# Two attention phases of a Trainium2 kernel: the score matmuls of a pair of heads on separate 64-row halves of the TensorE array

## The reference

```
q, k, v = heads(x @ Wq), heads(x @ Wk), heads(x @ Wv)     # 16 heads, width 8
scores  = q @ k.T / sqrt(8)          # layer 0: q, k turned by rope first
scores  = scores - slope[h] * (j - i), -inf where j > i   # layer 2 only
out     = softmax(scores) @ v
x       = x + out @ Wo
```

## Time and profile before

| what | value |
|---|---|
| time, median of 3 runs | 6658.86 us (6647.43 to 6664.04) |
| profiled execution, span from first to last instruction | 6645.5 us |
| TensorE matmul busy | 4915.4 us (74%) |
| VectorE busy | 4210.3 us (63%) |
| ScalarE busy | 2311.0 us (35%) |
| GpSimd busy | 1627.5 us (24%) |
| `rotary`: s1 of the first sequence to the last s2 | 205.6 to 1323.8 us |
| `alibi`: the same | 3910.1 to 4778.7 us |

### The profile page before, as it was taken

The page is one execution under the profiler, slowest core; times in us unless marked ns, Lnnn a source line. Parts: engine busy times, 40 slices in busy tenths (PEclk is TensorE's granted clock), DMA queues, the critical chain, the costliest instruction groups (busy, mean ns, idle before and its releaser), DMA issues. The chain is left out here.

```text
span 6645.5 us, 116690 instructions
## 1 busy us (share of the span) xinstructions
PE 4915.4 (74%) x40300; PEld 2948.5 (44%) x40521; DVE 4210.3 (63%) x9351; ACT 2311.0 (35%) x4383; POOL 1627.5 (24%) x1976
## 2 busy tenths in 40 slices
PE   3699999857671165675666649889766799897998
PEld 2233333233341154443334424444344577665776
DVE  7566666478897511487889846656499455455554
ACT  2366656620240001543001115555511344201443
POOL 1443333220233200033014423333244110001110
PEclk8899999988885555866777769999977899866999
DMA  1211121000132333410000022222000000000000
GB/s 37 45 41 36 34 44 32 17 5 0 38 120 77 75 93 75 90 33 28 0 0 0 0 41 52 47 47 47 17 0 0 18 0 0 1 0 0 1 0 26
DMA packets 230189, 202.36 MB, mean 30 GB/s; under 512 B 23551, under 2 KB 203863, under 8 KB 229335
## 3 DMA queue, kind: packets, MB, share of 16 engines
q1 hardware_dynamic: 229783, 196.88, 12.8%
HBM read 118.68 MB, written 72.88 MB: 29 GB/s over the span
## 5 line engine op out<-in xcount | busy, mean ns | idle before, releaser
L507 DVE TENSOR_REDUCE rotary_maxima<-rotary_ps_s 128x2 f32<-128x1024 f32 x512 | 616.6, 1220 | 418.0 <-PE rotary_ps_s L681 416.5
L730 ACT ACTIVATE rotary_probs<-rotary_ps_s 128x512 f32<-128x512 f32 x1024 | 555.5, 595 | 388.9 <-PE rotary_ps_s L697 373.9
L507 DVE TENSOR_REDUCE alibi_maxima<-alibi_ps_s 128x2 f32<-128x256 f32 (+3 forms) x512 | 412.4, 821 | 372.3 <-PE alibi_ps_s L684 369.2
L2017 DVE SCALAR_TENSOR_TENSOR x<-moe_ps_out,moe_weights,x 128x128 f32 (+1 forms) x1024 | 285.5, 344 | 461.0 <-PE moe_ps_out L2058 433.4
L2058 PEld LDWEIGHTS moe_ps_out<-w_moe_w,moe_hidden 128*128 128x128 f32 x4096 | 495.1, 192 | 108.5 <-issue 80.7
L730 ACT ACTIVATE alibi_probs<-alibi_ps_s 128x512 f32<-128x512 f32 (+3 forms) x1024 | 402.0, 439 | 344.9 <-PE alibi_ps_s L700 339.9
L2058 PE MATMUL moe_ps_out<-w_moe_w,moe_hidden 128*128 128x128 f32 x4096 | 500.6, 275 | 0.0
L2045 PE MATMUL moe_ps_hidden<-moe_z,w_moe_w 128*128 128x512 f32 x1024 | 490.0, 601 | 0.0
L2107 ACT ACTIVATE moe_hidden<-moe_ps_hidden,w_moe_b 128x512 f32<-128x512 f32 x512 | 345.4, 687 | 361.8 <-PE moe_ps_hidden L2045 350.2
L897 PE MATMUL moe_ps_experts<-w_moe_w,moe_normedT 128*128 128x512 f32 x512 | 302.3, 742 | 131.6 <-DVE moe_others L865 131.6
L697 PE MATMUL rotary_ps_s<-rotary_q_stack,rotary_k_stack 128*128 128x512 bf16 x1017 | 339.3, 392 | 30.5 <-ACT rotary_probs L730 7.3
(11 more groups left out here) (446 smaller groups left out, 10659.6 us busy)
## 6 DMA issues: line engine op xcount, KB each, us to landing
rotary_parts<-rotary_part SPq DMA_DIRECT2D x96, 128.0 KB, 2.2
rotary_q_stack<-rotary_parts SPq DMA_DIRECT2D x192, 64.0 KB
rotary_k_stack<-rotary_parts SPq DMA_DIRECT2D x192, 64.0 KB
convolve_bands<-in_filters SPq DMA_DIRECT2D x192, 64.0 KB, 2.7
alibi_parts<-alibi_part SPq DMA_DIRECT2D x96, 128.0 KB, 2.2
alibi_q_stack<-alibi_parts SPq DMA_DIRECT2D x192, 64.0 KB
alibi_k_stack<-alibi_parts SPq DMA_DIRECT2D x192, 64.0 KB
delta_n<-convolved SPq DMA_DIRECT2D x16, 256.0 KB, 2.0
```

The costliest lines, as they stand in the source:

```text
L507: v.tensor_reduce(maxima[:, blk, 2 * pair:2 * pair + 2], ps_s1[t % 2][:, :, 0:keys_of(blk)], AXIS.X, ALU.max).then_inc(s.max_made, 1)
L730: nc.scalar.activation(probs[u % 8][:, 0:T - lo], ps_s2[m][:, 0:T - lo], ACT.Exp).then_inc(s.exp_made, 1)
L2017: v.scalar_tensor_tensor(xb, ps_out[e % 2][:, b:b + 1, :], weights[par][:, b, e:e + 1], xb, ALU.mult, ALU.add).then_inc(s.added, 1)
```

## The change

The query stack gets one column block for each pair, like the key stack, with one head in rows 0 to 63 and the other in rows 64 to 127. Each score matmul of s1 and s2 then reads only the 64 rows of its head, from both stacks. In the causal phase s1's order changes: both heads' scores first, then both masks. The masks, pv and all items keep the full 128 rows. The loads into the query stack write the same bytes to adjacent blocks instead of every second block, and the stack is half as large.

```diff
-    qs = [ph.sb(f"q_stack{j}", [P, HEADS, T], BF16) for j in range(3)]
+    qs = [ph.sb(f"q_stack{j}", [P, PAIRS, T], BF16) for j in range(3)]
...
-                            to, part = ((qs[j][row:row + HD, two::2, :], Q_PARTS[n]), (ks[j][row:row + HD, :, :], K_PARTS[n]))[a]
+                            to, part = ((qs[j][row:row + HD, :, :], Q_PARTS[n]), (ks[j][row:row + HD, :, :], K_PARTS[n]))[a]
...
-                v.tensor_copy(qs[j][:], q_rows[:].unsqueeze(2).broadcast_to([P, HEADS, T])).then_inc(s.stack_set, 1)
+                v.tensor_copy(qs[j][:], q_rows[:].unsqueeze(2).broadcast_to([P, PAIRS, T])).then_inc(s.stack_set, 1)
...
                         for two in range(2):
-                            last = mm(ps_s1[t % 2][:, two, 0:n], qs[jb][:, 2 * pair + two, blk * P:(blk + 1) * P],
-                                      ks[jb][:, pair, 0:n], start=True, stop=not causal)
-                            if causal:
+                            rows = slice(two * ROWS, (two + 1) * ROWS)
+                            last = mm(ps_s1[t % 2][:, two, 0:n], qs[jb][rows, pair, blk * P:(blk + 1) * P],
+                                      ks[jb][rows, pair, 0:n], start=True, stop=not causal)
+                        if causal:
+                            for two in range(2):
                                 last = mm(ps_s1[t % 2][:, two, n - P:n], w.ident16, w.later_keys, start=False, stop=True)
...
+                        pair = 2 * qd + t % 2
                         for m in range(2):
-                            h = 4 * qd + 2 * (t % 2) + m
+                            rows = slice(m * ROWS, (m + 1) * ROWS)
...
-                            last = mm(ps_s2[m][:, 0:T - lo], ks[jc][:, h // 2, kb * P:(kb + 1) * P], qs[jc][:, h, lo:T],
+                            last = mm(ps_s2[m][:, 0:T - lo], ks[jc][rows, pair, kb * P:(kb + 1) * P], qs[jc][rows, pair, lo:T],
                                       start=True, stop=not causal)
```

More of the change, by code:

```diff
@@ L396, in attention @@
     oT = ph.sb("oT", [C, T])
-    q_rows = ph.sb("q_rows", [P, HEADS])
+    q_rows = ph.sb("q_rows", [P, PAIRS])
     carrier = ph.sb("pool_carrier", [1, 13])
@@ L437, in load_stack @@
                             row = two * ROWS + SHIFT_ROW
-                            sp.dma_start(qs[j][row:row + 3, two::2, :], zeros[:].rearrange("r (p t) -> r p t", t=T)).then_inc(s.stack_loaded, 16)
+                            sp.dma_start(qs[j][row:row + 3, :, :], zeros[:].rearrange("r (p t) -> r p t", t=T)).then_inc(s.stack_loaded, 16)
                 def store_shift(half):
@@ L448, in load_shift @@
                         row = two * ROWS + SHIFT_ROW
-                        sp.dma_start(qs[(j - 1) % 3][row:row + 3, half * PAIRS + two:(half + 1) * PAIRS:2, :],
+                        sp.dma_start(qs[(j - 1) % 3][row:row + 3, half * PAIRS // 2:(half + 1) * PAIRS // 2, :],
                                      shift_scratch[half].rearrange("m (p w) t -> w m p t", w=2)[two]).then_inc(shift_loaded[half], 16)
@@ L2473, in stack_rows @@
 def stack_rows(alibi):
-    q, keys = np.zeros((2, ROWS, HEADS), np.float32), np.zeros((2, ROWS, T), np.float32)
+    q, keys = np.zeros((2, ROWS, PAIRS), np.float32), np.zeros((2, ROWS, T), np.float32)
     keys[:, SHIFT_ROW:SHIFT_ROW + 3] = 1.0
@@ L2485, in stack_rows @@
                 for h in range(HEADS):
-                    q[h % 2, row, h] = -part[h]
+                    q[h % 2, row, h // 2] = -part[h]
                 keys[:, row] = (np.arange(T) % 256, np.arange(T) // 256 * 256)[m]
-    return q.reshape(P, HEADS), keys.reshape(P, T)
+    return q.reshape(P, PAIRS), keys.reshape(P, T)
 def host_arrays(v):
```

## The result

The changed kernel takes 6903.43 us (median of 4 runs, 6865.56 to 6939.4), the kernel before beside it on the same chip 6655.7 us. The ratio is 1.0379, with a 95% interval of 1.0352 to 1.0406: 248 us slower, where 81 us were forecast. The profiled execution has a span of 6909.9 us, 264.4 longer than before.

| phase | before | granted clock | after | granted clock |
|---|---|---|---|---|
| `rotary` | 205.6 to 1323.8: 1118.2 us | 0.97 | 199.4 to 1324.1: 1124.7 us | 0.90 |
| `alibi` | 3910.1 to 4778.7: 868.6 us | 0.98 | 3914.5 to 5040.6: 1126.1 us | 0.83 |

The account below looks back on a forecast made before the run. PE was taken to set the pace, partly waiting for exponentials. `alibi` +160, `rotary` -66 and set-up -13 gave +81 us on a span of 6645.5; with the median 13.4 above the span, 6740 us, range 6690 to 6800.

Parts of the forecast that it names:

- changes at about 0.1 us, pairs overlapped, clock kept: The forecast's own case for both attention phases: 6740 us, own range 6690 to 6800 us, 44% chance.
- a rival with 17%: Half arrays and frequent emptying lower PE's clock to 0.83: about +115 us in `alibi`, 6855 us; with part of `rotary` 6920.
- The price of a change: PE empties at each change of row count: 0.105 us into bf16, 0.20 into fp32; +307 us in `alibi`.
- the overlap: Two scores on different row halves run side by side, taken in full: saves 69 us in `alibi`'s s1, 0.21 us per `rotary` pair.
- the fill: Set-up of the q stack halves from 4.42 us to about 2.28, three times in each phase: -13 us.
- the rival's second number: The falling clock reaching part of `rotary` as well as `alibi`: 6920 us instead of 6855; chance of the whole rival 17%.
- The sign: In `alibi`'s timeline, about 0.15 us between a 64-row score's streaming end and the next start, six times a slot.
- `alibi` at kept clock: Changes of row count +307 us, s1's overlap -69, vanished waits for exponentials -78: together +160 us.
- The waits: PE's waits for exponentials in `alibi` vanish; 88.0 us for 14 sequences counted as 68, for 16 sequences -78 us.
- `rotary` at kept clock: Overlapped pairs less the changes at items gain 4.2 us a sequence, 66 us over 15.5 full rounds.
- The faster one: Changes between 64 and 128 rows in bf16 nearly free, at 0.04 us: 6575 us, 20% chance.
- Halves that don't overlap, and 64-row loads that aren't hidden: Slower rival in both phases: no overlap gives 6918 us, unhidden first weight loads behind changes 6895 us; 13% chance.

Follow-up runs that it names:

- one half in `rotary`: Both matmuls of each `rotary` pair on rows 0 to 63, second head's scores left out, `alibi` as in the kernel before: 6970.1 us, 1.0501.
- half masks: Against the kernel before, `alibi` with 128-row scores, masks over 64 rows only and the changed order of s1: 6868.54 us, 1.0314.
- own masks: Only `alibi` changed, each mask two 64-row matmuls on its head's rows: 6672.62 us, 1.0026, s2 issued as pairs; 6660.45 us, 1.0012, head by head.

## Why the prediction was wrong in size

**The step that failed** is "changes at about 0.1 us, pairs overlapped, clock kept": its last part. The sum took both phases at the clock of before and left the fall to a rival with 17%. The price of a change, the overlap and the fill held, as the next points show. At full clock a round of `alibi` is 8.5 us longer (60.4 against 51.85), times 15.5 full rounds 132 us; the phase grew by 257.5, so about 126 came with the clock (what is left after the rounds at full clock are taken off; with 16 rounds it is 121). The rival had put 115 on it. A round of `rotary` at full clock is 3.2 us shorter (64.25 against 67.48), some -50 us; the phase grew by 6.5, so some 56 came with the clock, where the rival's second number had 65. With -13 for the fill the sum at kept clock is 132 - 50 - 13 = +69, close to the +81 forecast; the clock's 182 on top, a remainder and not a measured term, give +251 (measured: 248 between the medians, 264 between the spans). The rival's 6920 us with both phases was the better number for 6903. That it came so close is partly luck: its clock of 0.83 was that of a feed-forward stretch, and no row tied it to `alibi`.

**Why the clock was misjudged.** The rival named half arrays and an engine that often empties as one cause and had no row that told them apart, since the earlier trace rows holds none with half arrays. The runs separate them: 96% busy on 64 rows gets 0.72; 97% busy with all the changes gets 0.95 with full-array scores and 0.83 with 64-row scores; full-array pairs added give 0.90 to 0.96 in `rotary`, and 0.83 to 0.93 in `alibi`. The time in which PE streams does not order them. An estimate from the traces (each matmul's columns at the granted clock, so longer at the lower level, and simultaneous ones counted once) gives 0.82 of the phase with one half in `rotary`, at a clock of 0.73, but 0.62 both with half masks, at 0.95, and with only `alibi` changed, at 0.83. In the changed kernel s1's pairs fill the array, but s2's scores stand alone on 64 rows with a mask behind each in `alibi`, and in `rotary` one by one behind exponentials in some 200 of 512 slots. The rest is not explained: half masks and own masks stay at 0.95 where it was 0.98 before; that PE's gaps have a part in it was not tested. Why rounds of the same instructions run at 1.00 and at 0.70 in one execution is not settled.

**The price of a change,** 0.105 us: the timeline has 0.103 after a 128-column score and 0.106 after a mask of s2. (The sign given for it, a gap of "about 0.15 us", does not fit the prediction's own price; 0.16 is the distance from start to start.)

**The overlap** of row halves, taken in full: s1's pair lasts as long as one matmul, and `rotary`'s pairs follow at 0.22 us.

**`alibi` at kept clock:** +160 us for 16 sequences were 10.0 a round, 8.5 measured. The waits had been counted at three quarters (68 of 88.0 us for 14 sequences); nearly all went (2.1 left), and at full size they make it 10.0 - 20/14 = 8.6. Price, overlap and waits so account for the round at full clock.

**`rotary` at kept clock:** -4.2 us a round forecast, -3.2 measured. The chain from s2 to pv kept its 1.87 us, the waits grew from 110.0 to 170.4, as said. Where the missing microsecond lies is not shown: the items' part of the sum was not taken apart, and the round of 64.25 is that of the kernel with repeated pairs, some of which may lie on the path (the changed kernel has no round at 1.00).

**The fill:** 2.28 us against 4.42, as forecast. The five kernels with the small stack in `rotary` load their first s1 there at 198.4 to 199.7 us, the six with the large one at 201.9 to 206.5: 6.4 us (three fills of 2.14) lie inside the 2.2 to 8.1 between them, and can't be read more closely.

**The other rivals.** The faster one would have needed changes below 0.08 us; the timeline's 0.103 and 0.106 exclude it, and so do 1081.6 us with the changes and 893.4 with none inside a slot, in the same phase. Halves that don't overlap, and 64-row loads that aren't hidden, are excluded by the timeline: the pair lasts as long as one, and steps in pairs are 0.22 us.

## What to carry to other kernels

Cutting the contraction to half of the array can pay only where two such matmuls run side by side, and by itself it gained nothing even there: `rotary` stayed at 0.9998, since the clock fell to 0.90, and own masks at 1.0012 and 1.0026, since PE then waited for the exponentials. Alone such matmuls stream as long as before, pay 0.1 us for each neighbour that uses all rows, and can lose the clock with the engine 96% busy. So price a change of array shape first by the number of changes between neighbours, and ask for the clock which rows work in each stretch. Where PE waits on a chain anyway, as in `rotary`, full-array work put into the waits can be worth its while: it gave 0.7%.

## What the runs showed of the hardware that was not expected

- The granted clock fell to 0.72 with PE busy 96% of 892 us on 64 rows, while the full array kept 0.98 at 92%.
- Redundant matmul pairs that fill both halves shortened a phase by 42 us (1122.1 to 1079.7) and raised its clock from 0.90 to 0.96; a third issue of the pair changed the kernel's time no further.
- Identical rounds of the changed `alibi` ran in 60.4 us at a clock of 1.00 and in 82.3 us at 0.70 within one execution.
- A matmul on one row half started ahead of earlier issued ones on the other half, in 311 of 512 slots of the kernel with own masks head by head.
